# Four edge loops of a graph network: steps in natural block order, each tile gathered once into a ring of 72 rows

## The reference, cut

```python
h = relu(layernorm(x));  x = x + L0(h)   # 8 heads: softmax attention over the edges of a node, two batch norms, a feed-forward
h = relu(layernorm(x));  x = x + L1(h)   # msg = h1[src] * (edge_attr_32 @ W_r2m.T + b) * C(edge_weight); sum by dst; two products
h = relu(layernorm(x));  x = x + L2(h)   # a = leaky(sum((h2[src] + edge_attr_128 @ We.T + be) * attn)); softmax by dst; sum of h2[src] * a; relu
h = relu(layernorm(x));  x = x + L3(h)   # msg = xw[src] * norm; sum by dst; relu(agg + b)
```

## Time and profile before

| | us |
|---|---|
| runs of the kernel before | 4839.44, 4834.09, 4837.98 (median 4837.98) |
| span of the profiled execution (its time is given by this span alone) | 4836.7 |
| e1, e2, e3: first gather | 1629.6, 2700.4, 3780.8 |
| busy of the span: PE / DVE / ACT / POOL | 3551.4 / 3365.7 / 2021.2 / 3211.3 |
| gathers of e1 to e3, 2496 | 2360.7 busy, 946 ns each |
| mean granted TensorE clock | 0.787 |

### The profile page before, as it was taken

How to read it: one execution, slowest core, us unless ns; L and a number is a source line. 1 busy time by engine, 2 the same in 40 slices (tenths; PEclk the granted TensorE clock), 3 DMA queues, 4 the chain that set the end, 5 groups by cost and what they waited for, 6 DMA issues and landing times. The chain is left out here.

```text
span 4836.7 us, 67940 instructions
## 1 busy us (share of the span) xinstructions
PE 3551.4 (73%) x13730; PEld 2548.5 (53%) x13730; DVE 3365.7 (70%) x9609; ACT 2021.2 (42%) x5849; POOL 3211.3 (66%) x3433
## 2 busy tenths in 40 slices
PE   8888777787798677767666578888888555555555
PEld 5566555565654455555555355555555444444444
DVE  7799999999833677777777477777777444444444
ACT  2466666666543433333333466666666000000000
POOL 1477777777200377777777577777777577777776
PEclk9866777867899878888888677777777677777777
DMA  3254454445300444444443244444443233333333
GB/s 118 89 139 136 138 139 138 139 138 139 90 16 3 119 122 127 125 125 125 126 125 108 80 111 113 114 114 114 114 114 109 80 111 112 112 112 112 111 112 100
DMA packets 346051, 540.75 MB, mean 112 GB/s; under 512 B 75816, under 2 KB 237899, under 8 KB 345675
## 3 DMA queue, kind: packets, MB, share of 16 engines
q0 software_dynamic: 146432, 386.15, 28.6%
q1 hardware_dynamic: 191755, 142.86, 10.3%
q10 hardware_dynamic: 7488, 7.72, 0.5%
HBM read 506.37 MB, written 30.07 MB: 111 GB/s over the span
## 5 line engine op out<-in xcount | busy, mean ns | idle before, releaser
L747 POOL DMA_INDIRECT e_rows<-table,src_idx x2496 | 2360.7, 946 | 1079.0 <-issue 538.8
L811 DVE TENSOR_TENSOR acc<-acc,banks 128x273 f32 (+3 forms) x3328 | 1298.9, 390 | 819.4 <-PE banks L799 646.0
L799 PE MATMUL banks<-e_rows,e_hot 128*128 128x128 f32 (+1 forms) x3328 | 990.0, 440 | 705.9 <-DMA e_rows<-table,src_idx 442.6
L799 PEld LDWEIGHTS banks<-e_rows,e_hot 128*128 128x128 f32 x3328 | 754.6, 256 | 935.1 <-DMA e_rows<-table,src_idx 484.6
L747 POOL DMA_INDIRECT edge_rows<-table,src_idx x832 | 800.5, 962 | 256.1 <-issue 188.5
L799 PE MATMUL banks<-edge_rows,e_hot 128*128 128x273 f32 x1664 | 728.3, 569 | 13.2 <-DVE edge_rows L1259 12.3
L799 PE MATMUL banks<-e_rows,e_weighted_hot 128*128 128x257 f32 x1664 | 645.5, 520 | 16.5 <-ACT e_weighted_hot L962 16.0
L926 ACT ACTIVATE e_apart<-const,dst_loc 128x128 bf16<-128x128 f32 x1664 | 505.9, 388 | 15.4 <-PEq L527 9.1
L799 PEld LDWEIGHTS banks<-edge_rows,e_hot 128*128 128x128 f32 x1664 | 385.9, 264 | 104.5 <-DVE acc L811 19.2
L799 PEld LDWEIGHTS banks<-e_rows,e_weighted_hot 128*128 128x128 f32 x1664 | 366.3, 249 | 108.3 <-issue 29.0
L962 ACT ACTIVATE e_weighted_hot<-e_hot,e_weight 128x128 f32<-128x128 f32 x832 | 254.3, 388 | 9.8 <-issue 1.1
(11 more groups left out here) (314 smaller groups left out, 4961.4 us busy)
## 6 DMA issues: line engine op xcount, KB each, us to landing
e_edge_in<-in_edge_attr SPq DMA_DIRECT2D x832, 80.0 KB
e_rows<-table,src_idx POOLq DMA_INDIRECT x2496
e_node_rows<-node_line SPq DMA_DIRECT2D x104, 256.0 KB, 3.4
edge_rows<-table,src_idx POOLq DMA_INDIRECT x832
table<-n_row SPq DMA_DIRECT2D x49, 132.0 KB, 1.7
table<-fn_row ACTq DMA_DIRECT2D x49, 129.0 KB
X<-in_x SPq DMA_DIRECT2D x1, 6272.0 KB
values<-table SPq DMA_DIRECT2D x49, 128.0 KB, 2.0
```

Of the source, the lines that this page charges most:

```text
L747: nc.gpsimd.indirect_dma_start(out=rows[:, u, q, 0:width], out_offset=None, in_=table, in_offset=bass.IndirectOffsetOnAxis(ap=at, axis=0)) ...
L799: nc.tensor.matmul(banks[:, 2 + q % turn, 0:width], onehot, rows, start=True, stop=True).then_inc(summed_tile, 1)
L811: nc.vector.tensor_tensor(at, at, banks[:, 2 + q % turn, 0:width], ALU.add).then_inc(added, 1)
```

## The change

**Order.** Blocks go round in natural order, from a starting block (`begin`: the block whose first tile lies furthest ahead of an even share, found on DVE by a reduction over all blocks); steps then run through the tiles in order too, and a border tile's two steps are neighbours. Two more dependent steps stand in DVE's chain, and POOL makes four lines of numbers in twelve dependent operations where one stood.

**Gathers.** In e1, e2 and e3 each tile is gathered once (`fetch_tiles`): 783 tiles, rounded up to 98 groups of 8, into a ring of HELD = 72 rows. `newest`, `needed` and `fresh` say which group a batch needs and whether it is new: six of the 104 batches need none. Gather g waits for the last step that can use row g - 72. The filters, logits and attributes of e1 are made per group, not per batch. PE reads a step's row by a slot from a register (`load_slots`, eight per batch). In e2 `value` adds in place for a new group, and takes the leaky maximum of each step's column by itself, at an address from a register; DVE reads 10 registers per batch and eight more (`fetch_places`) in a second load. e0 gathers as before; its rows' sources stay in `src_idx`.

**Where things lie.** X is in SBUF up to the end of `layer0_tail`; its blocks are stored to `nodes` in DRAM there. In e1 ACT's queue, in e2 SP's, loads a block four ranks ahead into a ring of five (`NodeRing`) and stores it when updated. In e3 all are loaded at the start, in seven DMAs of 7 blocks, and waited for at the first update. Sources and cutoffs by tile are turned on PE (seven transposes each, in the set-up and at block 44 of the first node stage), written twice behind one another to DRAM and loaded from the starting tile on. `pick_cutoff` is gone. The feed-forward's `hidden`, and e1's `hot` and `logit_part`, lie in parts of `acc`, which POOL clears afterwards.

```diff
+WORK = TILES + NB - 1
+FETCHED = TILES + 1
+FETCHES = -(-FETCHED // G)
+FETCH_W = FETCHES * G
...
+HELD = 72
...
+FETCH_RING = HELD // G
+SPARE = HELD - 2 * G
...
+ROW_REGS = G + 2 + G
...
+def newest(s):
...
+    at = min(s, WORK - 1)
+    ranks = -(-NB * (at + 1) // WORK) - 1
+    return at if ranks == 0 else at - ranks + 1
...
+def needed(j):
...
+    return newest(j * G + G - 1) // G
...
+def fresh(j):
...
+    if j >= BATCHES or j > 0 and needed(j) == needed(j - 1):
+        return None
+    return needed(j)
...
+def last_use(g):
...
+    return min(g + NB - 1, WORK - 1)
...
+        src_line = scratch("src_line", (P, TWICE), I32)
+        cutoff_line = scratch("cutoff_line", (P, TWICE))
...
-        X = sb(top, "X", [P, NB, D])
...
-        src_idx = sb(top, "src_idx", [P, STEPS], I32)
+        src_fetch = sb(top, "src_fetch", [P, FETCH_W], I32)
...
+                    now = step(v.scalar_tensor_tensor(size_key[:, :], first_tile[:, 0:NB], 64.0 * NB, prep_("lead_of"), ALU.mult, ALU.add))
...
+                    v.scalar_tensor_tensor(spread_all[:, 0, :], size_key[:, :], begin[:, 0:1], prefix[:, :], ALU.is_equal, ALU.mult, accum_out=begin[:, 1:2])
...
+                    v.tensor_tensor(begin[:, 3:4], begin[:, 1:2], begin[:, 2:3], ALU.subtract)
+                    v.tensor_scalar(own_steps[:, 2:3], own_size[:, 0:1], begin[0:NB, 1:2], float(WORK), ALU.is_lt, ALU.mult)
...
+                    pool.wait_ge(prep_in, 16)
+                    pool.wait_ge(idx_dve, at["begin"])
+                    link(g.tensor_scalar(line_a[at_tile, 0:FETCH_W], prep_("iota_k")[at_tile, 0:FETCH_W], begin[at_tile, 3:4], None, ALU.add))
+                    link(g.tensor_scalar(line_b[at_tile, 0:FETCH_W], line_a[at_tile, 0:FETCH_W], float(TILES), -float(TILES), ALU.is_ge, ALU.mult))
+                    link(g.tensor_tensor(line_a[at_tile, 0:FETCH_W], line_a[at_tile, 0:FETCH_W], line_b[at_tile, 0:FETCH_W], ALU.add))
+                    link(g.tensor_copy(fetch_tile, line_a[at_tile, 0:FETCH_W]))
+                    steps = slice(0, BATCHES * G)
+                    pool.wait_ge(idx_dve, at["block"])
+                    link(g.tensor_scalar(line_a[at_slot, steps], block[at_slot, steps], begin[at_slot, 2:3], float(TILES), ALU.is_lt, ALU.mult))
+                    link(g.tensor_tensor(line_b[at_slot, steps], line_a[at_slot, steps], tile_k[at_slot, steps], ALU.add))
+                    link(g.tensor_scalar(slot_line, line_b[at_slot, steps], begin[at_slot, 3:4], None, ALU.subtract))
+                    link(g.tensor_scalar(line_a[0:1, steps], block[0:1, steps], begin[0:1, 2:3], float(TILES), ALU.is_lt, ALU.mult))
+                    link(g.tensor_tensor(line_b[0:1, steps], line_a[0:1, steps], tile_k[0:1, steps], ALU.add))
+                    link(g.tensor_scalar(line_a[0:1, steps], line_b[0:1, steps], begin[0:1, 3:4], float(FETCH_W - 1), ALU.subtract, ALU.min))
+                    fetch_at = batch_row[:, :, FETCH_AT:FETCH_AT + G]
+                    for to, of in ((slice(0, BATCHES - 2), slice(2, BATCHES)), (slice(BATCHES - 2, BATCHES), slice(0, 2))):
+                        link(g.tensor_copy(fetch_at[:, to, :], line_a[0:1, steps].rearrange("p (n q) -> p n q", q=G)[:, of, :]))
...
+                    for g in range(GROUPS):
+                        last = nc.tensor.transpose(banks[:, 4 + g // 4, g % 4 * P:(g % 4 + 1) * P], end_f[:, 1, g, :], ident)
+                    last.then_inc(src_turned, 1)
...
+                        def keep_twice(line, tiles):
+                            sp.dma_start(line[:, 0:TILES], tiles[:, 0:TILES]).then_inc(tiles_out, 16)
+                            sp.dma_start(line[:, TILES:TWICE], tiles[:, 0:FETCH_W]).then_inc(tiles_out, 16)
...
+                        sp.wait_ge(src_tiles_ready, 1)
+                        keep_twice(src_line, src_tiles)
...
+                            if b == 44:
+                                pe.wait_ge(cut_steps, 6)
+                                for g in range(GROUPS):
+                                    last = nc.tensor.transpose(banks[:, 6 + g // 4, g % 4 * P:(g % 4 + 1) * P], cut[:, g, :], ident)
+                                last.then_inc(cut_turned, 1)
...
+                        def keep_cutoffs():
+                            dve.wait_ge(cut_turned, 1)
+                            v.tensor_copy(cut_tiles, banks[:, 6:8, :].rearrange("p b c -> p (b c)")[:, 0:GROUPS * P]).then_inc(cut_tiles_ready, 1)
...
+        def fetch_tiles(pool, table, width, rows, fetched, summed_tile, spare_read=()):
+
+
+            for g in range(FETCH_W):
+                if g == SPARE:
+                    for read, count in spare_read:
+                        pool.wait_ge(read, count)
+                if g >= HELD:
+                    pool.wait_ge(summed_tile, summed(0, last_use(g - HELD)))
+                nc.gpsimd.indirect_dma_start(out=rows[:, g % HELD, 0:width], out_offset=None, in_=table,
+                                             in_offset=bass.IndirectOffsetOnAxis(ap=src_fetch[:, g:g + 1], axis=0)).then_inc(fetched[g // G % FETCH_RING], 16)
+            for n in range(FETCHES - FETCH_RING, FETCHES):
+                pool.wait_ge(fetched[n % FETCH_RING], landed(n, FETCH_RING))
+
+        def load_slots(j):
+
+            return nc.values_load_multi_w_load_instructions(
...
+                if self.with_fetch:
+                    self.fetch_at = fetch_places((n + 2) % BATCHES)
...
-                        def sums_of(j, u, q):
...
-                        def pick_cutoff():
...
+                                by, row = weighted_hot[:, u % 2, q, :], rows[:, bass.ds(slots[q], 1), 0:sum_w].squeeze(1)
+                            sum_tile(pe, j, q, by, row, summed_tile, added, sum_w)
...
                         if many:
-                            pick_cutoff()
...
+                            slots = None if many else load_slots(j)
                             for q in range(2):
-                                sums_of(j, u, q)
...
+                        def value(n, u, fetch_at=None):
+
                             if many:
+                                dve.wait_ge(gathered[u], arrived(n, u))
                                 dve.wait_ge(logit_ready, n + 1)
                                 v.tensor_tensor(val[:, :].rearrange("p (t h) -> p t h", t=G), rows[:, u, :, D:ROW0],
                                                 at_dst[:, :].rearrange("p (t h) -> p t h", t=G), ALU.max).then_inc(val_ready, 1)
-                            else:
-                                v.tensor_tensor(sums[:, 0, :].unsqueeze(2), rows[:, u, :, D + 1:D + 2], edge_q[:, bass.ds(n * G, G)].unsqueeze(2), ALU.add).then_inc(logit_ready, 1)
-                                dve.wait_ge(logit_ready, n + 1)
-                                v.scalar_tensor_tensor(val[:, :], sums[:, 0, :], slope, sums[:, 0, :], ALU.mult, ALU.max).then_inc(val_ready, 1)
+                                return
+                            m = fresh(n)
+                            if m is not None:
+                                dve.wait_ge(gathered[m % FETCH_RING], landed(m, FETCH_RING))
+                                logits = edge_q[:, m * G:(m + 1) * G]
+                                slots = rows[:, m % FETCH_RING * G:(m % FETCH_RING + 1) * G, D + 1:D + 2].squeeze(2)
+                                v.tensor_tensor(logits, slots, logits, ALU.add).then_inc(logit_ready, 1)
+                                dve.wait_ge(logit_ready, m + 1)
+                            for q in range(G):
+                                logit = edge_q[:, bass.ds(fetch_at[q], 1)]
+                                last = v.scalar_tensor_tensor(val[:, q:q + 1], logit, slope, logit, ALU.mult, ALU.max)
+                            last.then_inc(val_ready, 1)
...
+                        value(0, 0, None if many else fetch_places(0))
...
-                rows = sb(st, f"{tag}_rows", [P, RING, G, width])
-                hot = sb(st, f"{tag}_hot", [P, 2, G, P])
...
+                    logit_part = unsummed[:, 2 * G:3 * G, :]
+                    we, attn = rows[:, SPARE:SPARE + 2, :], rows[:, SPARE + 2:SPARE + 4, :]
...
+                        fetch_tiles(pool, table, width, rows, fetched, summed_tile, ((we_attn_ready, 1), (node.w2_ready, 2)) if filtered else ())
+                        if filtered:
+                            pool.wait_ge(logits, FETCHES + RING)
+                            pool.wait_ge(summed_tile, summed(BATCHES - 1, G - 1))
+                            nc.gpsimd.memset(unsummed[:, 0:3 * G, :], 0.0)
 
...
-                            turns(load)
-                            for u in range(RING):
-                                sp.wait_ge(edge_ready[u], 16 * G * TURNS)
+                            for n in range(FETCHES):
+                                load(n, n % RING)
...
-                                scale_radial(j + 2, (r + 2) % RING, r % 2)
+                            two = fresh(j + 2)
```

(56 more changed lines are left out.)

356 lines of the change are left out of this document (203 added, 153 removed).

## The result

The changed kernel takes 4998.27 us (median of 4 runs, 4995.15 to 5000.83) where the kernel before takes 4838.65: ratio 1.0332, 95% interval 1.0317 to 1.0347. The profiled execution has a span of 4997.3 us, 160.6 more than the 4836.7 of before.

What follows compares the result with a forecast made beforehand. POOL's gathers were taken to pace e1, e2 and e3, with DVE nearly as tight in e2. Terms -51 (e3), -41 (e1), +109 (e2) and +8 (before the loops) sum to +25, giving 4863 us, range 4832 to 4904.

Steps and rivals of the forecast that it cites:

- e3, -51: Loop e3: 48 fewer gathers save 60 us, two batches after the last landing cost 6.3, node loads 3: -51 us.
- e1, -41: Loop e1: fewer gathers, partly offset by PE's register loads and ACT's delay; 9.6 us per batch, -41 us.
- everything covered: Loop e1's favourable bound: all added work hidden, -60 + 6 = -54 us.
- (a) value, +1.0: Loop e2 on DVE: an add plus eight 128x1 multiply-max at register addresses, +1.0 us per batch (0.74 to 1.54).
- (b) registers, +0.6: Loop e2 on DVE: 10 and 8 registers in two loads instead of 12 in one, +0.6 us per batch (0.2 to 1.0).
- (c): Loop e2 on PE: slot load and eight addresses, some 1.2 us, covered by waiting for DVE: cost 0, uncovered up to 1 us a batch.
- e2's bounds: Loop e2 paced by DVE between 10.4 us per batch (+41) and 12.0 us (+206), around 11.1 us (+109).
- The front, +8: Before the loops: set-up block +4 us, node stage +4 us, last tail stage 0; +8 us (4 to 20).
- R2: Registers and addresses are dear: e2 at 11.7 us per batch (+171), e1 bound by PE's loads (-20); 4946 us, chance 0.20.
- R3: The ring holds: all three loops stay with POOL at 9.42 us per batch; 4684 us, chance 0.03.
- R4: Slots stall the gathers: eight come 10 us late at a loop's start, three times, +30; 4890 us, chance 0.03.
- R5: No less work for POOL: a gather interval grows by as much as the count falls; chance 0.02.

Runs made afterwards that it cites:

- aligned12: Changed kernel with rows of 12 numbers again, fetch places on a line of their own, both loads beginning at multiples of 16 bytes: 4875.97 us, 1.008 of before.
- one_op: aligned12 with e2's value as one 128x8 operation, without picking each step's column; the second register read dropped out too: 4725.93 us, 0.9767 of before.
- shift8: Kernel before with only its line of rows moved by 8 bytes, so every row of 12 begins between multiples of 16: 4956.08 us, 1.0241 of before.

## Why the prediction was wrong

- **e3, -51.** Right: -54.9. The term of two batches after the last landing was 6.3 us, measured 22.4 against 17.1 us from last gather to end, 5.3.
- **e1, -41.** Near: -32.8. From first to last the gathers took 977.9 us, so PE's load and ACT's DMAs did not stop POOL; what was lost is the lag at the end, where POOL's last gather and the memset stand 38.50 us apart and e2's first gather comes after another 18:

```profile
2610.99 0.94 POOL L877 DMA_INDIRECT e_rows<-table,src_fetch  x1 [0.30 <-issue]
2650.43 2.67 POOL L1570 MEMSET acc<- 128x3072 f32 x1 [38.50 <-PE banks L941]
2671.12 0.95 POOL L877 DMA_INDIRECT e_rows<-table,src_fetch  x1 [18.01 <-POOLq L199]
```

aligned12 shows whose lag it was: DVE's reads, a term that I had in e2 and not in e1. There e1 takes 1018.0 us (1633.3 to 2651.3), 53 less than before, which is the bound "everything covered"; the price that I had put on PE's reads does not show.
- **e2, (a) value, +1.0.** Right in size: 1.38 us for 0.43 in the 98 batches with a new group, +0.95, and 0.84, +0.41, in the six without. The sum as written, 0.21 + 8 x 0.15 + 0.2 - 0.43, is 1.18; the 1.0 and both of its bounds leave out the 0.2, 18 us over e2. The eight take 0.99 us with their spacing of 0.12 in the mean, the lower bound rather than my 0.15:

```profile
L1321 DVE SCALAR_TENSOR_TENSOR e_val<-edge_q x832: 143/159/234, 2683.4 to 3958.6; 128x1 f32 x167
```

- **e2, (b) registers, +0.6.** This is the step that failed: it measured 324.6 - 97.5 = 227 us, +2.2 us per batch. "About 0.07 us a register and 0.25 fixed" was drawn from DVE's idle time around reads that all begin on a multiple of 16 bytes; the queue's own rows of before say it more exactly, 0.596 us for eight and 0.856 for twelve. The change moved every second row off such a multiple, and the trace of before has no row for that. Of the 2.2 us, 1.1 go with the place of the rows (aligned12) and 1.1 are the second read, with what the first took longer beside it. With 2.2 in place of 0.6 the forecast's own sum gives 9.5 + 1.0 + 2.2 = 12.7 us per batch; measured 12.38. e2's stretch came out 136 us longer than forecast, and the whole kernel 135: of this aligned12 gives back 104 in e2 by the place of the rows alone, and the rest is put down to the second read by its durations.
- **e2, (c).** Right for the changed kernel: PE waits for DVE, 243 us in 900, so its slot reads are covered. What they cost without that cover was not shown.
- **e2's bounds.** "10.4 us (+41) and 12.0 us (+206)" count from 10.0 us per batch, the +109 from 10.04; 4 us lie between.
- **The front, +8.** +3.5.
- **Rivals.** R2 is what happened, with an e2 of 12.38 us where I had put 11.7 and an upper bound of 12.0: "up to 1.0 if the second load pays in full" took one load's price at its old place as the ceiling. Its other half, an e1 bound by PE's loads, did not occur. The page I set beside it, the Trainium skill (Runtime: NRT & Kernel Launch, Instruction fetch mechanics), gives some 200 ns per register, told of loads from HBM; the reads from SBUF that begin 8 bytes off come near it (2.735 us for twelve, 0.23 each), the others do not (0.07 each). The small instructions started 0.12 us apart, not at the estimated 0.06 us that follows from the 58 cycles plus elements of the Trainium skill (VectorE: DVE Perf Modes, the section on the TRN2 errata); the trace does not agree. R3 did not occur, and would not have with both terms gone: in one_op POOL is never held up, but e2 still takes 9.88 us per batch instead of 9.42. R4 and R5 did not occur.

## What to carry to other kernels

Registers read from SBUF in an inner loop have a price that hangs on the address: keep the record that one load reads a multiple of 16 bytes long and beginning on one (twelve numbers took 0.85 us begun so, ten 1.06), and look for these loads in the queue's own view, since no busy share counts them. Before gathers are saved in a loop, ask what the next engine has to spare per batch; here 0.5 us per batch on DVE stood against 60 us saved on POOL, and the same saving paid nearly in full in e3 (55 us), came with 245 us more in e2, and showed as some 14 us there once DVE's two terms were gone (one_op). Where one stage can't afford the new addressing, convert its data to the old order in a stage with an idle engine.

## What was not expected of the hardware

- A read of eight registers takes 0.60 us begun on a multiple of 16 bytes and 1.86 begun 8 bytes off it, one of ten 1.06 or 2.30, one of twelve 0.85 or 2.73; one of twenty, begun on it, takes 1.35. For the twelve shift8 shows that nothing but the 8 bytes does it. Other starts, 4 or 12 bytes off, were not tried. The tens of the changed kernel's e1, of both kinds:

```profile
L907 DVEq TENSOR_LOAD <-lines x103: 1057/1087/2319, 1653.5 to 2630.5; - x103
```

- In aligned12's e2 the reads of twelve and eight take 1.07 and 0.81 us, each 0.2 more than alone; in the changed kernel's pairs the second takes 0.61, as alone. The cause was not found.
- The kernel before is 16 to 18% slower on four other chips, at the same 0.95 us per gather instruction, and a gain of 2% is gone on the one where it was tried. The cause was not found.
